# Second norm taken into the linear attention, softmax sums inverted once, the first expert's weights rounded from step 25

## The reference, cut to what matters

```python
x = L0_attn_x
xn = layernorm(x)
x = x + attn0(xn) + ffn0(xn)
xn = layernorm(x)
x = x + attn1(xn) + ffn1(xn)

def attn0(xn):
    q, k, v = split(xn @ Wqkv + bqkv)
    scores = q @ k.T * scale + alibi_causal
    return (softmax(scores) @ v) @ Wo + bo
def ffn0(xn):
    return out0 * mask0 + out1 * (1.0 - mask0)
def attn1(xn):
    q, k, v = silu(xn @ Wq), silu(xn @ Wk), silu(xn @ Wv)
    o = lightning_attn(q, k, v, log_decay)
    o = rmsnorm(o * sigmoid(xn @ Wg1 @ Wg2)) * norm_w
    return o @ Wo
def ffn1(xn):
    return bitlinear(sigmoid(bitlinear(xn, w1)) * bitlinear(xn, w2), w3)
```

## Time and profile before

| | |
|---|---|
| median of 3 runs | 2032.83 us (2027.39 to 2034.8) |
| the profiled execution | 2035.95 us, span 2034.1 us |
| mean granted TensorE clock | 0.907 |
| TensorE busy | 1698.3 us, 83% of the span |
| VectorE, ScalarE, GpSimd busy | 981.8, 586.3, 645.3 us |

### The profile page before, as it was taken

The page is one execution under the profiler, slowest core; times in us unless marked ns, Lnnn a source line. Parts: engine busy times, 40 slices in busy tenths (PEclk is TensorE's granted clock), DMA queues, the critical chain, the costliest instruction groups (busy, mean ns, idle before and its releaser), DMA issues. The chain is left out here.

```text
span 2034.1 us, 22765 instructions
## 1 busy us (share of the span) xinstructions
PE 1698.3 (83%) x8338; PEld 1103.0 (54%) x8338; DVE 981.8 (48%) x1582; ACT 586.3 (29%) x806; POOL 645.3 (32%) x527
## 2 busy tenths in 40 slices
PE   6996499999999999994445999923999996499997
PEld 5883244444444444442334777712776774378886
DVE  7654356656666666633544555544334435022222
ACT  3120054434444444452111221223233232022221
POOL 4000357588687680001113666612001001000000
PEclk9996589989999999997767999955999998789999
DMA  7758234453446443003432112165102201612210
GB/s 238 245 186 185 29 94 116 91 148 100 92 131 144 99 121 68 11 17 119 150 129 84 58 58 63 55 219 202 42 1 84 83 1 42 227 68 83 82 41 21
DMA packets 108804, 204.71 MB, mean 101 GB/s; under 512 B 27914, under 2 KB 42010, under 8 KB 106826
## 3 DMA queue, kind: packets, MB, share of 16 engines
q1 hardware_dynamic: 80830, 131.72, 22.4%
q0 software_dynamic: 13648, 51.61, 8.5%
q10 hardware_dynamic: 14224, 20.02, 2.9%
HBM read 134.10 MB, written 68.96 MB: 100 GB/s over the span
## 5 line engine op out<-in xcount | busy, mean ns | idle before, releaser
L924 DVE TENSOR_REDUCE att_maxes<-att_unit 128x1 f32<-128x512 f32 (+3 forms) x640 | 386.0, 611 | 290.9 <-PE att_unit L794 177.7
L906 ACT ACTIVATE att_probs<-att_scores 128x1024 f32<-128x1024 f32 (+1 forms) x320 | 285.5, 895 | 373.2 <-PE att_scores L823 187.5
L840 PE MATMUL att_outp<-att_probs,att_vs 128*64 128x512 f32 (+3 forms) x1280 | 308.8, 562 | 0.0
L794 PE MATMUL att_unit<-moew_wbh,moew_wah 100*128 100x512 f32 (+2 forms) x320 | 152.3, 492 | 9.4 <-DMA moew_wbh<-alibi_k_rounded 4.9
L1509 PE MATMUL glu_u<-glu_xh,glu_w 128*128 128x512 f32 x352 | 138.9, 395 | 18.9 <-DMA glu_xl<-zn_lo 18.9
L794 PE MATMUL att_unit<-moew_wbl,moew_wal 100*128 100x512 f32 (+2 forms) x320 | 138.3, 439 | 0.6
L1510 PE MATMUL glu_u<-glu_xl,glu_w 128*128 128x512 f32 x352 | 138.4, 393 | 0.0
L823 PE MATMUL att_scores<-moew_wah,moew_wbh 102*128 102x512 f32 (+2 forms) x320 | 110.2, 417 | 28.4 <-ACT att_probs L906 28.4
L794 PEld LDWEIGHTS att_unit<-moew_wbh,moew_wah 100*128 100x128 f32 x320 | 67.2, 212 | 121.5 <-DVE att_maxes L924 80.7
L794 PEld LDWEIGHTS att_unit<-moew_wbl,moew_wal 100*128 100x128 f32 x320 | 60.2, 190 | 117.0 <-DVE att_maxes L924 81.7
L267 PE MATMUL proj_acc<-moew_woh,proj_ath 128*128 128x512 f32 x64 | 32.9, 513 | 97.4 <-DVE proj_atl L1097 97.4
(11 more groups left out here) (274 smaller groups left out, 3543.9 us busy)
## 6 DMA issues: line engine op xcount, KB each, us to landing
att_q_raw<-in_w POOLq DMA_DIRECT2D x48, 352.0 KB, 3.9
w_ternary<-att_q_out POOLq DMA_DIRECT2D x24, 352.0 KB, 2.6
glu_w<-w_ternary ACTq DMA_DIRECT2D x9, 768.0 KB, 11.7
xn<-qkv_x SPq DMA_DIRECT2D x4, 1024.0 KB, 6.7
q_hi<-qkv_hi SPq DMA_DIRECT2D x16, 256.0 KB, 3.2
q_lo<-qkv_lo SPq DMA_DIRECT2D x16, 256.0 KB, 3.7
k_hi<-qkv_hi SPq DMA_DIRECT2D x16, 256.0 KB, 2.6
k_lo<-qkv_lo SPq DMA_DIRECT2D x16, 256.0 KB, 3.3
```

The source lines that it names most:

```text
L794: last = pe.matmul(unit[:, h, 0:cover], qs[par][0:SROWS, h, t * P:(t + 1) * P], ks[par][0:SROWS, h, g * CH:g * CH + cover], start=True, st ...
L840: last = pe.matmul(outp[v_cols(h), c % 2, off:CH], vs[p % 2][:, kt, v_cols(h)], probs[:, g % 4, h, off:CH], start=kt == 0, stop=kt == TT * ...
L906: act.activation(probs[:, g % 4, :, off:CH], scores[:, g % 2, :, off:CH], ACT.Exp).then_inc(exped, 1)
L924: dve.tensor_reduce(maxes[:, h, t, g:g + 1], unit[:, h, 0:width], AX.X, ALU.max).then_inc(unit_taken, 1)
```

## The change

Three parts.

1. In attention the 16 roundings on ScalarE stand at steps 25, 27, ... 55. GpSimd's list is the same.
2. The sums are stored as one row per head. The projection sets a tile `inv` of 128x512 to ones, loads the 16 rows of the four chunks in it at partitions 0, 32, 64 and 96, inverts it once, and TensorE spreads the inverses over the 32 partitions of each head by float32 products with a matrix of ones and zeros, from the host (`widen`: 4 matmuls of 256 columns per half chunk, from partitions `c*32` to `c*32+16` of both operands). VectorE multiplies with the PSUM result. SP asks for `at` of half n+2 as soon as the low part of half n is there, ahead of the wait for the additions; the identity matrix for the experts is loaded here.
3. The stage of the second norm is gone. The linear attention loads x, takes statistics, normalizes, and TensorE transposes the tiles (`norm_turn`) in the same ring, for chunk 0 at the start and for chunk c+1 behind the gate product of chunk c; ScalarE makes the high and VectorE the low part, and SP stores both for the gated unit. The output product of the chunk before stands behind these transposes. The weights are loaded by SP in tiles that serve another purpose later (`y`, `kd`), and split by ScalarE and GpSimd in chunk 0.

```diff
+        SPLIT_FROM = 25
-                if g % 2 and g // 2 < len(ahead):
-                    ws.hi(act, g // 2)
+                if g >= SPLIT_FROM and g % 2 and (g - SPLIT_FROM) // 2 < len(ahead):
+                    ws.hi(act, (g - SPLIT_FROM) // 2)
...
+            sp.wait_ge(cleared, 1)
+            for c in range(NCH):
+                sp.dma_start(inv[c * QUAD:c * QUAD + NH, :], sum_d[:, c * CH:(c + 1) * CH]).then_inc(sum_in, 16)
+            load_att(0)
+            load_att(1)
+            load_rows(0)
+            load_rows(1)
             for n in range(NHC):
+                if n + 2 < NHC:
+                    load_att(n + 2)
                 sp.wait_ge(added, (n + 1) * PER)
                 sp.dma_start(half_rows(out_d, n), y_half(n)).then_inc(stored[n % 2], 16)
                 if n + 2 < NHC:
-                    load(n + 2)
+                    load_rows(n + 2)
...
+            def widen(n):
+                c, s = n // 2, slice(n % 2 * HC, (n % 2 + 1) * HC)
+                heads = slice(c * QUAD, c * QUAD + NH)
+                if n >= 2:
+                    pe.wait_ge(scaled, n - 1)
+                for k in range(KT):
+                    last = pe.matmul(wide[n % 2][:, k, :], spread[heads, k, :], inv[heads, s], start=True, stop=True)
+                last.then_inc(widened, 1)
...
-                dve.reciprocal(su[n % 2][:], su[n % 2][:]).then_inc(inverted, 1)
-                dve.wait_ge(inverted, n + 1)
-                dve.tensor_tensor(at[n % 2][:], at[n % 2][:], su[n % 2][:], ALU.mult).then_inc(scaled, 1)
+                dve.wait_ge(widened, n + 1)
+                dve.tensor_tensor(at[n % 2][:], at[n % 2][:], wide[n % 2][:], ALU.mult).then_inc(scaled, 1)
...
-def second_norm_stage(nc, cst_d, x_d, zh_d, zl_d, pieces):
...
+            def norm_turn(c):
+                for t in range(TT):
+                    out = slot("norm", c, t)
+                    pe.wait_ge(norm.normed, c * TT + t + 1)
+                    for k in range(KT):
+                        last = pe.transpose(out[:, k * P:(k + 1) * P], x[:, t, k * P:(k + 1) * P], ident)
+                    last.then_inc(made, 1)
...
                 last.then_inc(made, 1)
+                if c + 1 < NCH:
+                    norm_turn(c + 1)
+                if c:
+                    output(c - 1)
                 gates(c)
...
             for h in range(NH):
+                if h == NH // 2:
+                    act.wait_ge(zeroed, 2)
+                    norm.take_root(act, 0)
                 act.activation(pair_decay[:, h, :], dist, ACT.Exp, scale=ld_f[:, h:h + 1]).then_inc(expd, 1)
...
+            split(("q",))
+            norm_high(0)
+            split(("k",))
             for c in range(NCH):
...
+                if c + 1 < NCH:
+                    norm.take_root(act, c + 1)
                 if c:
                     take_root(c - 1)
+                else:
+                    split(("v", "g1"))
...
+                if c + 1 < NCH:
+                    norm.stats(dve, c + 1, chunk_in(c + 1))
                 if c:
                     invert(c - 1)
...
                     normalize(c - 1)
+                if c + 1 < NCH:
+                    norm.normalize(dve, c + 1)
+                    norm_low(c + 1)
+                if c:
                     add_output(c - 1)
```

More of the change, by code:

```diff
@@ L1744, in output @@
             def output(c):
+                if c == 0:
+                    ws.wait(pe)
                 pe.wait_ge(lo_ready, (c + 1) * KT)
@@ L1811, in _ @@
             pe.wait_ge(zeroed, 2)
+            norm_turn(0)
             for c in range(NCH):
-                pe.wait_ge(x_in, c * 32 + 32)
+                wait_taken(pe, "norm", c, TT - 1)
+                if c == 0:
+                    ws.wait(pe, KT)
                 for m in range(KT):
@@ L1925, in normalize, with first_tile, chunk_in, norm_low @@
                                       ALU.subtract).then_inc(lo_ready, 1)
+            def first_tile(t):
+                dve.wait_ge(first_in[t], 16)
+            def chunk_in(c):
+                return lambda t: dve.wait_ge(x_in, c * 16) if t == 0 else None
+            def norm_low(c):
+                for t in range(TT):
+                    s = slice(t * P, (t + 1) * P)
+                    dve.wait_ge(norm.xh_ready, c * TT + t + 1)
+                    dve.tensor_tensor(xl[:, :, s], arrived(dve, "norm", c, t).rearrange("p (k n) -> p k n", n=P),
+                                      xh[:, :, s].bitcast(F32), ALU.subtract).then_inc(taken["dve"], 1)
             def add_output(c):
```

204 lines of the change are left out of this document (99 added, 105 removed).

## The result

| | before | the change |
|---|---|---|
| median | 2030.54 us (2027.39 to 2034.8, 4 runs) | 1882.43 us (1882.01 to 1884.51, 4 runs) |
| profiled execution's span | 2034.1 us | 1882.9 us |
| mean granted clock | 0.907 | 0.946 |

A forecast was written before the change was run, and what follows sets the result against it. No engine was full in the projection, so waits set its time; removing TensorE's waits was worth their whole time. Terms -34 - 78 - 43 - 1 = -156 from 2035.95 gave 1880, put at 1878 for the median; range 1860 to 1908.

The forecast's parts named there:

- Term A: Attention: moving the roundings removes TensorE's 28.4 us wait and 5.8 us of half clock; -34 us, bounds -28.4 and -37.
- Term C: Second norm and linear attention: first q product 56.4 us earlier, less added waits and transposes; -43 us, bounds -49 to -30.
- Without a wait I keep the high clock: Attention: with the wait gone, TensorE would not fall to half clock for 11.6 us, saving 5.8 us.
- Term B: Projection: one short inversion, spreading by TensorE, pitch 7.7 us instead of 17.8; -78 us, bounds -51 and -81.
- fifth transfer: Projection start: `su`, taken as fifth in the old list, landed 11.0 us in; sums that late would add 5.7 us.
- Rival 1: Projection stays a loop of loads with a pitch of 11.2 us; 27 us more, 1905; chance 0.10.
- What stood against it: Linear attention: +3 us for chunk 0's k products waiting on weight rounding, +10.5 for transposes in chunks 0 to 2.
- Term D: One barrier fewer and the experts' identity matrix loaded earlier; -1 us.
- 2: Rival: in linear attention the norm a chunk ahead holds others up; 21 us more, about 1900; chance 0.10.
- 3: Rival: in attention the piece isn't there at step 25 and the wait returns; 1912 if all of it; chance 0.03.
- 4: Rival: GpSimd's list ends after attention, costing time beyond 140 us of delay; over 2036 past 296; chance 0.02.

The follow-up runs named there:

- e16: The whole change with spreading products made twice, the first of the two taking all 128 rows of both operands instead of 16; 1911.41 us.
- e8: The whole change with the inverses split into high and low parts, spread by two rounded products in place of one in float32; 1894.3 us.
- e4: The whole change, but SP asks for the attention output of half n+2 behind the store of half n, as before; 1910.26 us.
- e7: The whole change with every spreading product made twice over, the second overwriting the first; 1928.1 us.
- e14: The whole change with the roundings at steps 25 to 39 and 51 to 65, pausing during the next pair's loads; 1891.18 us.
- e13: The whole change run again, unaltered, on the chip of the variants; 1894.19 us.
- e3: The kernel before with only the second norm moved into the linear attention; 1985.14 us.
- e5: The whole change with the 16 roundings back at steps 1 to 31; 1906.52 us.
- e15: e14 with TensorE turning the rows' maxima one unit later and ScalarE rounding v and gate weights behind its first two takes of k; 1889.21 us.

## Why the prediction was right, and where it was off

The forecast was 4 us from the median of the result, and its range holds the later result (1894.19) too. That closeness is in good part luck. Of the three large terms two came out beyond the bounds that the prediction gave them, to opposite sides: A with -26.2 (bounds -28.4 and -37) and C with -50.8 (bounds -30 and -49). The prediction had put its failure as a whole at just that, two terms beyond their bounds; it did not think of two that cancel. The sum itself, 2035.95 - 156 - 3.1, makes 1877 and not 1878. Point by point:

- **Term A, -34, measured -26.2, and 12 to 18 by later runs.** "So the wait of 28.4 goes whole" held for the wait. The step that failed is the other one, "Without a wait I keep the high clock": in the change's profile TensorE ran twelve microseconds at 1.2 GHz all the same, and in the others the clock rose at 223 to 229 and was lost again at the stop behind it. Why it rose early in some and at 239 in one stays open, and so does what the stop is. What the forecast didn't have at all: the roundings now fall on the loads for the next pair (steps 40 on), and something stands between 228 and 246 that the old wait had covered. That the roundings "keep to ScalarE's slack" was read from an average over the stage and overlooked the place. It was also read from the wrong column: the 423.2 us of the earlier trace rows are VectorE's, ScalarE is busy for 312.5.
- **Term B, -78, measured -75.2.** Pitch 7.60 (7.7 forecast), spreading 1.99 (1.9), and the rest behind the last first product as forecast within 1 us. The mis-sized term is the start: the sums took 8.6 us and not 5.3, which I had called an estimate with 5.7 to be added at worst. The "fifth transfer" there is a misreading: the first inversion before waited for the loads of the first half chunk alone, and its `su` was the second transfer asked for. So even a second transfer had landed only 11.0 us in. On `widen` the trace decides for the upper end, 2 us serial and not 0.57. The Trainium skill (TensorE: Matmul & The Clock Gate, "Why this matters for your kernels") had said so, and e16's two rows (453 ns with 16 rows, 447 with 128) agree with it.
- The loop of loads was described over two half chunks, and for the change that is right (e8's 7.68). Rival 1's price of 27 us came from "everything but the inversion stays in the loop", a pitch of 11.2; e4 shows what that would have been, 10.7 and 19.5 us.
- **Term C, -43, measured -50.8.** The path to the first q product was 23.8 for 23.5. What stood against it was 5.2 for 13.5, but not because its terms were too high. The wait ahead of k was 1.7 (3 forecast), and the transposes of a chunk cost some 2.6 us at full clock and 1.1 of waits, 11 us in three chunks where 10.5 were forecast. So these two make 12.6, and 7.4 came back from what the forecast had left as it was. Most of that is the products of this stage, each 6 to 7 ns faster, some 5 us together; some 1 us is the clock, which rose 4 us behind the first q product and not 6; the rest I can't place. So the step of the sum that failed is the one it does not name, that the other products keep their price. No run tells why they did not. The table loads did not show on the path. ScalarE's timeline around the root leaves no room for a drain:

```profile
1245.57 1.28 ACT L318 ACT_TABLE_LOAD   x1
1246.86 0.30 ACT L318 ACTIVATE lin_ln_root<-lin_ln_mv,lin_eps 128x4 f32<-128x4 f32 x1
1247.18 1.28 ACT L1883 ACT_TABLE_LOAD   x1
```

The Trainium skill (ScalarE: Activation LUTs, "What `ACT_TABLE_LOAD` costs") adds 1.38 us for it to each 1.28; the rows show 0.01 to 0.02, and the measurement decides.
- **Term D**: -0.2 for -1.
- Errors of +8 in A, +3 in B and -8 in C cancelled in the main, and the error in C itself is a gain that nobody had foreseen. The sum was better than its parts, and that was luck.

The rivals: 1 and 2 did not occur; 3 (the wait returns) did in a small form, as late pieces; 4's mechanism was real, and its threshold lay at 108 us of delay, not 140.

## What to carry over

When a long wait is removed, look at what stood beneath it on the other engines, and at what the moved work now falls on: place by place, not against the average slack of the stage. When a sum comes out right, check its terms all the same; here two of three had left their bounds. When a loop has a load in it, follow each engine's own order to see over how many rounds the loop goes; e4's 5 us became 19.5 by that alone. A shortened operation is worth what it takes from the loop only down to the next equal bound, here 7.6 us on both sides.

## What the runs showed of the hardware

- Products with 16 rows can lower the clock although TensorE has no gap: in e7, with some 3.7 us of them in each 11.5, it was 0.81 to 0.84, and 0.66 in one stretch; in the change, with 2.0 in each 7.6, it was 1.00, and in e16, where half of e7's spreading products took 128 rows, 1.00 as well. The duration of a product is the same for 16 and 128 rows (453 and 447 ns an instruction in e16).
- A gap of 1.5 to 2.4 us in a dense stretch was in several profiles followed by some 3 to 10 us at one half (1.50 and 2.02 us before 296.8 and 624.8 in e8, 1.89 before 750.9 in the change, 2.44 before 502.8 in e14), and in others by nothing (1.77 before 297.1 in e13, 2.01 before 758.5 in e16). What decides is not shown. Such a fall costs half its length, 2 to 5 us, an estimate; that it is what makes the same kernel differ from run to run is likely and not shown.
- The same product in fp32r, 128 rows and 512 columns, came every 0.233 us in the linear attention before and every 0.227 in the change and in e3, e5, e13, e15 and e16, both at full clock.
- The same kernel gave 1882.4 and 1894.2 us at two times between which the kernel before differed by 4 us. A part whose worth lies between 7 and 26 us can't be sized from one pair of profiles.
